# A table of products of weights, built through DRAM and then built on TensorE alone

## What is computed

```python
def _cin_layer(x0, x, kernel):
    W = kernel.reshape(m, h_prev, kernel.shape[1])
    return jnp.einsum('bmd,bhd,mho->bod', x0, x, W)
x = x0
finals = []
for k in (k1, k2, k3):
    x = _cin_layer(x0, x, k)
    finals.append(jnp.sum(x, axis=-1))
logit = jnp.concatenate(finals, axis=-1) @ kf
```

## Time and profile before

| | us |
|---|---|
| median of 3 runs (311.8 to 312.88) | 311.81 |
| the profiled execution | 312.8 |
| span of its instructions | 311.0 |
| PE busy in the span | 294.1 |
| POOL, DVE, ACT busy | 221.9, 196.8, 179.2 |
| contractions (L568) | 228.7 |

### The profile page before, as it was taken

One profiled execution on the slowest core, in us unless ns is written; L12 is line 12 of the kernel. 1 busy time (PEld: TensorE's weight loads), 2 busy tenths in 40 slices (PEclk: granted clock), 3 DMA queues, 4 the chain that ended last, 5 costly groups with the idle time before them and its releaser, 6 DMA issues.

```text
span 311.0 us, 7703 instructions
## 1 busy us (share of the span) xinstructions
PE 294.1 (95%) x3018; PEld 84.2 (27%) x3018; DVE 196.8 (63%) x215; ACT 179.2 (58%) x195; POOL 221.9 (71%) x131
## 2 busy tenths in 40 slices
PE   7249989999999999999999999999999999999995
PEld 2032322222222222222222222222222222222231
DVE  0555657766665667766665667776665667776631
ACT  1336537756574756766574756766574756677511
POOL 0334877969698797969697896979697896979700
PEclk9756999999999999999999999999999999999999
DMA  6998999999998969799697979799797979620100
GB/s 210 401 346 243 386 365 355 383 394 327 415 301 357 301 266 342 309 315 334 273 307 270 301 268 329 301 334 329 283 300 278 297 269 316 257 70 2 34 2 1
DMA packets 18632, 86.86 MB, mean 279 GB/s; under 512 B 3899, under 2 KB 4155, under 8 KB 9915
## 3 DMA queue, kind: packets, MB, share of 16 engines
q1 hardware_dynamic: 15880, 78.10, 68.5%
q10 hardware_dynamic: 2707, 8.57, 11.2%
q0 software_dynamic: 32, 0.00, 0.0%
HBM read 86.13 MB, written 0.53 MB: 279 GB/s over the span
## 4 chain that ended last, share of the span: by engine, by line
PE 87%; DMA 5%; DVE 3%; ACTq 2%; ACT 1%; issue 1%; POOL 1%; SPq 0%; POOLq 0%
PE acc L568 69%; PE acc L576 10%; PE rot L554 8%; DMA feat<-u_rows 3%; DMA u<-k3p 2%; ACTq L336 1%; DVE split L465 1%; DVE prod L490 1%; ACT prod L287 0%; ACT split L299 0%; ACTq L191 0%; POOL split L400 0%; PE acc L584 0%; PE acc L622 0%; ACT ysb L304 0%
## 5 line engine op out<-in xcount | busy, mean ns | idle before, releaser
L568 PE MATMUL acc<-prod,w 128*32 128x512 f32 x2048 | 228.7, 598 | 4.2 <-ACT prod L287 2.9
L390 POOL TENSOR_TENSOR prod<-u,v 128x1024 f32<-128x1024 f32 x64 | 152.6, 2385 | 23.2 <-PE acc L568 17.3
L568 PEld LDWEIGHTS acc<-prod,w 128*32 128x32 f32 x2048 | 63.5, 110 | 152.4 <-issue 135.3
L490 DVE TENSOR_TENSOR prod<-rot,u 128x1024 f32<-128x1024 f32 x64 | 77.7, 1215 | 6.3 <-PE rot L554 4.4
L287 ACT ACTIVATE prod<-rot 128x1024 f32<-128x1024 f32 x64 | 65.2, 1021 | 24.8 <-PE rot L554 17.4
L496 DVE TENSOR_TENSOR xy<-acc,ysb 128x512 f32<-128x512 f32 x32 | 22.1, 691 | 89.3 <-ACT ysb L304 89.3
L490 DVE TENSOR_TENSOR prod<-rot,v 128x1024 f32<-128x1024 f32 x64 | 77.6, 1213 | 0.0
L304 ACT ACTIVATE ysb<-acc,kf 128x512 f32<-128x512 f32 x32 | 22.0, 687 | 84.3 <-PE acc L576 54.0
L291 ACT ACTIVATE feat<-u 96x2048 f32<-96x2048 f32 x32 | 60.9, 1903 | 0.0
L396 POOL TENSOR_TENSOR low<-xc,split 128x512 f32<-128x512 f32 x30 | 35.1, 1170 | 32.7 <-ACT split L295 32.7
L400 POOL TENSOR_TENSOR split<-low,split 128x512 bf16<-128x512 f32 x30 | 34.9, 1164 | 5.0 <-ACT split L299 4.7
(11 more groups left out here) (35 smaller groups left out, 21.6 us busy)
## 6 DMA issues: line engine op xcount, KB each, us to landing
u<-u_rows SPq DMA_DIRECT2D x30, 1024.0 KB, 4.9
v<-v_rows SPq DMA_DIRECT2D x30, 1024.0 KB, 8.7
xc<-x_chunks SPq DMA_DIRECT2D x32, 256.0 KB, 10.0
feat<-u_rows ACTq DMA_DIRECT2D x30, 256.0 KB, 7.4
u<-u_rows SPq DMA_DIRECT2D x4, 512.0 KB, 11.7
v<-v_rows SPq DMA_DIRECT2D x4, 512.0 KB, 12.8
u<-k3p SPq DMA_DIRECT2D x2, 512.0 KB, 5.4
...
```

The lines of the kernel that those rows point to most:

```text
L390: nc.gpsimd.tensor_tensor(prod[p][:, UV, pair(half)], us[n][:, pair(half)], vs[n][:, pair(half)], ALU.mult).then_inc(uv_ready, 2)
L490: nc.vector.tensor_tensor(prod[p][:, t, pair(half)], rot[:, pair(half)], r[n][:, pair(half)], ALU.mult).then_inc(products_ready, 1)
L568: mm = nc.tensor.matmul(acc[p][h][quad(c), :], w[:, t, h * G:(h + 1) * G], prod[p][:, t, chunk(c)], start=(t == first), stop=(first is Non ...
```

## The change

T is made in another layout and never leaves the core. TensorE multiplies `k2s` (as weights, 32 columns for each c) by `vk`: 32 matmuls of 64 columns give T with g on the partitions, four values of c side by side in the four groups of 32 partitions (`t_ps`). VectorE and ScalarE copy it in four pieces (`place_t`) to `tt`, a table of 95 x 64 places in the second buffer of `prod`; it holds zeros elsewhere, which GpSimd fills in with one MEMSET of 6080 elements as its first instruction. A weight table of a tile is a diagonal of `tt`, read in steps of 65 elements. `tables_of_t` uses each diagonal (`diagonal`) as weights against a 32 x 32 unit matrix, and so gathers, transposes and adds left and right in PSUM (`sum_ps`): 54 matmuls of 32 columns. One ScalarE copy puts the sum in `w`. The diagonal for the single squares and the linear part are gathered by two more such matmuls in `fold(1)`.

The code of slabs 0 and 1 is changed along with it. All fixes come before the first contraction, slab 1's rotation comes after the whole x1 half of slab 0, and slab 1's products and slab 2's split are made in step 0 as in the loop. Slab 1 is split by GpSimd. `xc` of slab 0 is loaded ahead of `k2t`, `pick` ahead of `kf`; the loads of slabs 1 to 3 have a new order, and no DMA of the table is left on SyncE, ScalarE or GpSimd.

```diff
-WRAP = 2 * M
+WRAP = 2 * M - 1
+ORDERS = (FIRST, {t: pair[::-1] for t, pair in FIRST.items()})
-                fold[q, i, m] += 1
+                fold[q, i, m] -= 1
+        tt = prod[1][:, UW:, :].rearrange("p t n -> p (t n)")[:, 0:(M + WRAP) * 2 * M]
+        t_places = tt.rearrange("p (c a) -> p c a", a=2 * M)
-        vt_ps, v_ps = acc[0][1][:, 0:H1], acc[1][1][:, 0:M]
-        t_ps = [acc[0][1][2 * M * n:2 * M * n + M + 1, :] for n in range(2)]
+        vt_ps, v_ps, t_ps = acc[0][1][:, 0:H1], acc[1][1][:, 0:WRAP], acc[0][0]
+        sum_ps = acc[1][1][:, P:2 * P].rearrange("p (t g) -> p t g", g=G)
+        def diagonal(pair, q, turn):
+            (c, dc), (a, da) = pair
+            at = ((0 if turn else M) + c + dc * q) * 2 * M + a + da * q
+            return tt[:, at:at + (M - 1) * (2 * M + 1) + 1:2 * M + 1]
+        def place_t(copy, n):
+            for j in (2 * n, 2 * n + 1):
+                copy(t_places[quad(j), M + j:2 * M:Q, :], t_ps[quad(j), :].rearrange("p (c a) -> p c a", a=2 * M)
+                     ).then_inc(tt_ready[n], 1)
...
+            load_xc(0, 0)
             sp.dma_start(k2s, k2t).then_inc(k2_in, 16)
-            load_xc(0, 0)
             sp.dma_start(k1s[:], k1g).then_inc(k1_in, 16)
...
             load_halves(0, 0)
+            load_halves(1, 1)
+            place_fields(sp, 0, 0)
+            load_halves(1, 0)
             load_xc(2, 2)
-            place_fields(sp, 0, 0)
-            load_halves(1, 1)
-            load_halves(1, 0)
+            load(2, 2)
             place_fields(sp, 1, 1)
-            sp.wait_ge(t_out, 32)
-            sp.dma_start(tl[:, UW, :], table(*FIRST[UW])).then_inc(t_in, 16)
-            sp.dma_start(tr[:, UW, :], table(*FIRST[UW][::-1])).then_inc(t_in, 16)
-            sp.dma_start(tl[:, WW, :], table(*FIRST[WW])).then_inc(t_in, 16)
-            sp.dma_start(tr[:, WW, :], table(*FIRST[WW][::-1])).then_inc(t_in, 16)
-            load(2, 2)
             load_xc(3, 3)
+            sp.wait_ge(t_ready, 1)
             load(3, 3)
...
-            act.dma_start(vk[:, M:M + 1], kf[M:M + H1, :]).then_inc(kf2_in, 16)
+            act.dma_start(pick32[:], pick).then_inc(pick_in, 16)
+            act.dma_start(vk[:, WRAP:], kf[M:M + H1, :]).then_inc(kf2_in, 16)
...
             act.dma_start(kf1[:], bass.AP(tensor=kf.tensor, offset=0, ap=[[0, CHUNKS], [1, M], [1, 1]])
                           ).then_inc(kf1_in, 16)
-            act.dma_start(pick32[:], pick).then_inc(pick_in, 16)
             act.wait_ge(xc_in[0], 16)
             split_high(0, 0, 0)
+            split_mid(0, 0)
             act.wait_ge(t_ready, 1)
-            nc.scalar.copy(ts[:, CHUNK:], t_ps[1]).then_inc(ts_ready, 1)
-            act.wait_ge(ts_ready, 2)
-            store_t(act, 0)
-            store_t(act, 1)
-            split_mid(0, 0)
+            act.wait_ge(tt_cleared, 1)
+            place_t(nc.scalar.copy, 1)
+            act.wait_ge(rot_ready, 1)
+            square_w(0, 0, 0)
             act.wait_ge(xc_in[1], 16)
             split_high(1, 1, 1)
-            split_mid(1, 1)
-            act.wait_ge(rot_ready, 1)
-            square_w(0, 0, 0)
             act.wait_ge(products_ready, 2)
             square_w(0, 0, 1)
-            act.wait_ge(xc_in[2], 16)
-            split_high(2, 0, 2)
-            act.wait_ge(t_out, 32)
-            act.dma_start(tl[:, VW, :], table(*FIRST[VW])).then_inc(t_in, 16)
-            act.wait_ge(cleared, 2)
-            act.dma_start(tr[0:HALFWAY.start, VW, :], table(*FIRST[VW][::-1], count=Q - 1)).then_inc(t_in, 16)
-            act.dma_start(tl[:, UV, :], table(*FIRST[UV])).then_inc(t_in, 16)
-            act.dma_start(tr[:, UV, :], table(*FIRST[UV][::-1])).then_inc(t_in, 16)
-            act.wait_ge(cleared, 1)
-            act.dma_start(wf[quad(3), :], ts[M:M + 1, :]).then_inc(lin_in, 16)
+            act.wait_ge(sum_ready, 1)
+            nc.scalar.copy(w[:, :, G:2 * G], sum_ps).then_inc(w_ready[1], 1)
+            split_mid(1, 1)
             for half in range(2):
                 act.wait_ge(first_in[0][half], 32)
-            split_mid(2, 0)
             square_fields(0, 0, 0)
             act.wait_ge(kf1_in, 16)
...
-                    if not isinstance(s, int) or 1 <= s < SLABS - 2:
+                    if not isinstance(s, int) or s < SLABS - 2:
...
+            nc.gpsimd.memset(tt, 0.0).then_inc(tt_cleared, 1)
             pool.wait_ge(k1_in, 16)
-            add_tables(0, k1s[:, 0:TILES, :], k1s[:, TILES:2 * TILES, :])
+            nc.gpsimd.tensor_tensor(w[:, :, 0:G], k1s[:, 0:TILES, :], k1s[:, TILES:2 * TILES, :], ALU.add
+                                    ).then_inc(w_ready[0], 1)
             for half in (1, 0):
                 pool.wait_ge(first_in[0][half], 32)
                 multiply_uv(0, 0, half)
-            pool.wait_ge(t_out, 32)
-            pool.dma_start(td[quad(2), :], bass.AP(tensor=t_tab.tensor, offset=0,
-                                          ap=[[(WRAP + 1) * G, M], [1, G]])).then_inc(td_in, 16)
-            split_low(2, 0, 2)
-            split_last(2, 0)
-            pool.wait_ge(t_in, 16 * 8)
-            add_tables(1, tl[:], tr[:])
+                if half == 1:
+                    split_low(1, 1, 1)
+            split_last(1, 1)
...
-            dve.wait_ge(t_ready, 1)
-            nc.vector.tensor_copy(ts[:, 0:CHUNK], t_ps[0]).then_inc(ts_ready, 1)
             split_low(0)
             dve.wait_ge(pick_in, 16)
             nc.vector.tensor_copy(picks[:], pick32[:]).then_inc(picks_ready, 1)
             split_last(0)
+            dve.wait_ge(t_ready, 1)
+            dve.wait_ge(tt_cleared, 1)
+            place_t(nc.vector.tensor_copy, 0)
             dve.wait_ge(rot_ready, 1)
             multiply_w(0, 0, 0, (1,))
             subtract_fixes(0)
-            split_low(1)
             multiply_w(0, 0, 0, (0,))
-            split_last(1)
-            fold_squares(0, quad(0), k1s[quad(0), 2 * TILES, :])
-            dve.wait_ge(rot_ready, 2)
-            multiply_w(1, 1, 1, (1,))
             subtract_fixes(1)
-            dve.wait_ge(td_in, 16)
-            fold_squares(1, quad(2), td[quad(2), :])
-            multiply_w(1, 1, 1, (0,))
+            dve.wait_ge(wf_cleared, 1)
+            dve.wait_ge(fold_ready[0], 1)
+            nc.vector.tensor_tensor(wf[quad(0), :], k1s[quad(0), 2 * TILES, :], fold_ps[0], ALU.add
+                                    ).then_inc(wf_ready[0], 1)
+            dve.wait_ge(fold_ready[1], 1)
+            nc.vector.tensor_copy(wf[2 * M:, :], rest_ps).then_inc(wf_ready[1], 1)
...
+            def tables_of_t():
+                for t in range(TILES):
+                    parts = [[(order[t], turn) for n, order in enumerate(ORDERS) if (n, t, q) != (1, VW, Q - 1)
+                              for turn in range(1 + (order[t][0][0] + order[t][0][1] * q > 0))] for q in range(Q)]
+                    for k in range(max(len(of) for of in parts)):
+                        for q, of in enumerate(parts):
+                            if k < len(of):
+                                mm = nc.tensor.matmul(sum_ps[quad(q), t, :], diagonal(of[k][0], q, of[k][1]),
+                                                      kzs[:, 2 * M:3 * M], start=(k == 0), stop=(k == len(of) - 1),
+                                                      skip_group_check=True)
+                mm.then_inc(sum_ready, 1)
             def fold(h):
                 pe.wait_ge(fixed[h], 2)
-                nc.tensor.matmul(fold_ps[h], fixs[:, 4 * P:], w[:, WW, h * G:(h + 1) * G], start=True, stop=True
-                                 ).then_inc(fold_ready[h], 1)
+                mm = nc.tensor.matmul(fold_ps[h], fixs[:, 4 * P:], w[:, WW, h * G:(h + 1) * G], start=True,
+                                      stop=(h == 0), skip_group_check=True)
+                if h == 1:
+                    nc.tensor.matmul(fold_ps[1], diagonal((ZERO, ZERO), 0, 0), kzs[:, 2 * M:3 * M], start=False,
+                                     stop=True, skip_group_check=True)
+                    mm = nc.tensor.matmul(rest_ps[M:, :], t_places[:, M:2 * M, WRAP], kzs[:, 2 * M:3 * M], start=True,
+                                          stop=True, skip_group_check=True)
+                mm.then_inc(fold_ready[h], 1)
...
-            nc.tensor.matmul(v_ps, vts[:], kzs[:, 2 * M:], start=True, stop=True).then_inc(v_done, 1)
+            nc.tensor.matmul(v_ps, vts[:], kzs[:, 2 * M:2 * M + WRAP], start=True, stop=True).then_inc(v_done, 1)
             pe.wait_ge(v_ready, 1)
             pe.wait_ge(kf2_in, 16)
             pe.wait_ge(k2_in, 16)
-            for n in range(2):
-                mm = nc.tensor.matmul(t_ps[n], vk[:], k2s[:, n * CHUNK:(n + 1) * CHUNK], start=True, stop=True)
+            for c in range(M):
+                at = c // Q * 2 * M
+                mm = nc.tensor.matmul(t_ps[quad(c % Q), at:at + 2 * M], k2s[:, c * G:(c + 1) * G], vk[:],
+                                      start=True, stop=True, skip_group_check=True)
```

(17 more changed lines are left out.)

71 lines of the change are left out of this document (25 added, 46 removed).

## The result

The changed kernel takes 308.83 us (median of 5 runs, 308.59 to 309.75), the kernel before 311.81 beside it. The ratio is 0.9912, with a 95% interval of 0.9885 to 0.9938: 3.0 us or 1% less. The same two kernels, run again on another occasion, gave 308.35 (6 runs) against 312.15 (11 runs), ratio 0.9876 (0.9848 to 0.9904). The ratios leave out an execution that lies over 1.5% above the fastest of its kernel; here that is a single one, the profiled execution of e_fill. The forecast was 6.1 us less, so the direction was right and the size was twice too large.

The account below looks back on a forecast made before the run. TensorE was taken as the bound, busy from 50 us on, with gains only ahead of the loop: slab 1's contraction 4.8 us earlier and 1.3 from the feature row, minus 6.1, giving 305.7 us; range 303.5 to 312.3.

Parts of the forecast that it names:

- The waits of 5.5 and 2.9 us: TensorE's waits for VectorE's last split of slab 0 (5.5) and ScalarE's squares of slab 0 (2.9): both forecast to go.
- the wait ahead of rotate(2): Ahead of slab 1's contraction: TensorE waits for GpSimd's split of slab 2, forecast as 1.9 us.
- the wait on the feature row: TensorE's wait of 1.3 us behind 43 us for the DMA of slab 2's feature row: forecast to go.
- the chain of the split: Split of slab s + 2 hangs on the rotation of s + 1: 6.5 us from rotation's end to GpSimd's split_last.
- The price of a small matmul: T and tables: 0.026 us from record to record; 0.052 for the tables at 1.2 GHz.
- the range of 6.4 to 13.9: GpSimd's MEMSET of 6080 elements: bounds from VectorE's MEMSET and GpSimd's product; lower end taken, hidden by loads and T.
- what is late next. A new wait of 1.9 us: Step before rotate(2): slab 2's split comes at 31.3, TensorE is done at 29.4, slab 1's contraction begins at 32.1.
- The baseline: Whole kernel: profiled execution 312.8 us, median 1.0 below it at 311.81; the forecast for the median starts from 311.8.
- R1: Start: tables and fixes don't bring back 2.4 GHz; clock stays down until the contractions; 311.6 us, chance 0.19.
- R2: Tables: diagonal weights read slowly, 0.052 us a record at 2.4 GHz, 0.104 at 1.2; 309.9 us, shared chance 0.17.
- R3: GpSimd's MEMSET takes 13.9 us, so place_t and tables start later: +2.5, 308.2 us; shared chance 0.17.
- R4: Start: DRAM trip was covered (0.2 us), TensorE only gets 54 more matmuls; no chance beyond R1's.

Follow-up runs that it names:

- e_fill: Changed kernel with 12 matmuls of 512 columns on zeros in TensorE's wait ahead of rotate(2): median 307.89 us (8 runs).
- e_xc2: Changed kernel with the load of slab 2's xc put ahead of slab 1's halves: 308.69 us (7 runs).
- e_shift: Changed kernel with 20 matmuls of 32 columns on zeros ahead of the first matmuls of V: 308.76 us (4 runs).
- e_copy: Changed kernel with TensorE's code 19 instructions shorter ahead of the tables and ScalarE's copy of their sum ahead of its second square of slab 0: 308.74 us.
- e_xc2_fill: Changed kernel with slab 2's xc loaded ahead of slab 1's halves and 8 matmuls on zeros ahead of rotate(2): 307.69 us, ratio 0.9862 to the kernel before.
- e_split2: Changed kernel with slab 2's xc loaded ahead of slab 1's halves and slab 2 split ahead of the loop: 307.62 us, ratio 0.9857 to the kernel before.
- e_all: Changed kernel with the edits of e_split2 and e_copy together: 307.12 us (6 runs), ratio 0.9859 to the kernel before.
- e_few_tables: Changed kernel with only 16 of the 54 matmuls of the tables: 307.85 us (4 runs).
- e_before: The kernel before, unedited, profiled again: profiled execution 312.55 us, median of 14 runs beside it 311.74.

## Why the prediction was half right

*What held.* The waits of 5.5 and 2.9 us went, the wait ahead of rotate(2) came, the wait on the feature row went, and where xc was there in time the chain of the split took 6.4 us from rotation to rotation, as read from the loop (e_xc2, e_shift, e_copy). The rows foretold slab 1's contraction at 32.1, and it came at 32.52. That it came so near is luck: TensorE reached the wait at 28.5 instead of 29.4, stood 0.8 longer and then took 0.6 longer in rotate(2).

*What cancelled on the way.* T began at 8.9 (9.8 forecast) and took 1.10 us and not 1.9: 64 records at 0.013 us each, half the lower bound. The tables took 3.8 us and not 4.5, but made up otherwise: 99 records in 1.99 us at 1.2 GHz, 0.020 each where 0.052 was taken, and a gap of 1.5 us that no row had announced. The price of a small matmul was taken from sixteen records with 128 columns, 0.026 us; with 64 columns it is 0.013, and with the 32 columns of the tables 0.019 to 0.020 at either level of the clock, so columns alone don't set it. The MEMSET took 5.16 us, below the range of 6.4 to 13.9. The clock fell once in slab 0's first contraction (5.24 us for 29 records), where I had it back for good.

*The step that failed* is "what is late next. A new wait of 1.9 us". It was priced as idle time alone. In the trace of before, a wait of TensorE was followed by 1.2 GHz; the prediction used that for the start and forgot it for the wait that it had itself added. It cost 0.6 us in rotate(2) and 1.15 in the contraction. The wait was also 0.8 longer, because ScalarE's split had to wait for slab 2's xc, which landed at 25.8, behind slab 1's halves, and which I had not checked. Of eight profiles in which TensorE stood empty for 1.8 to 3.2 us between 27 and 33 us, seven show the slow level right behind; e_copy, with 1.82 us, does not, and why is open. The four in which that wait was filled or gone (e_fill, e_xc2_fill, e_split2, e_all) all keep 2.4 GHz. In whole executions this price can hardly be seen: those four lie 0.9 to 1.7 us below 308.83 and 0.5 to 1.2 below 308.35, but so does e_few_tables, 307.85, which has the slow stretch, and e_copy, without it, gains nothing.

*The sum.* At the features of slab 1 the changed kernel was ahead by 45.46 - 40.60 = 4.9 us instead of 6.1. It ends ahead by 311.0 - 306.8 = 4.2. The 0.7 in between went in the loop, where the prediction held that nothing in the change touches the work: 4.85 were left at rotate(5) (64.74 against 59.89), 4.48 at rotate(6) (72.50 against 68.02), which waited 0.30 us for GpSimd's split and did not before, and the rest went in steps of under 0.1. Behind rotate(5) ScalarE's two issues of feature rows start 0.59 us after its copy of y ends, and its first square 0.81 after the rotation; before it was 0.21 and 0.43. That is the size of the step, and why the issues come late was not tried. The loss is no accident of one execution: from the start of rotate(3) to the end of the span it is 263.6 or 263.7 us in both profiles of the kernel before, and 264.2 to 264.4 in all eleven of the changed kernel and those made from it. All that they differ in lies ahead of rotate(3).

*The baseline.* The last 1.2 us, from 4.2 by the profiles to 3.0 by the medians, is no property of the edit: the profiled execution of before lay 1.0 above its median (0.8 in e_before), that of after 0.2 below. The forecast moved both by the same 1.0. On the second occasion the medians differed by 3.8. So of the 3.1 us by which 6.1 was too much, some 1.2 are the clock and the longer wait, less what the early start gave back, 0.7 the loop, and 1.2 the reading of a profiled execution as a typical one. The last share is the least certain.

*The rivals.* R1 (1.2 GHz until the contractions) did not come about: PEclk is 0.50, 1.00, 0.50 and 1.00 again by 22 us. R2 (slow diagonals) fell as a price: a record took 0.020 us at 1.2 GHz, where R2 had 0.104. Loads of weights with steps of 65 elements took a median of 163 ns there, against 164 for neighbours. But at 2.4 GHz the diagonals are slower. The last two of these lines are e_xc2_fill's loads for T, which read neighbours, and for its tables, both at that level:

```profile
L569 PEld LDWEIGHTS acc<-kzs,prod x108: 133/163/189, 12.0 to 15.6; 128*32 128x32 f32 x108
```

```profile
L616 PEld LDWEIGHTS acc<-vk,v x64: 106/110/110, 8.9 to 9.8; 128*32 128x32 f32 x64
L570 PEld LDWEIGHTS acc<-kzs,prod x108: 133/158/168, 11.9 to 15.9; 128*32 128x32 f32 x108
```

So 158 ns against 110, and 0.018 us from record to record (1.81 us for 99) where T, with twice the columns, has 0.013. The diagonals hardly gain from the higher clock; by an estimate from these rows that is some 108 x 0.005 or 0.5 us. The Trainium skill (SBUF — State Buffer, Door 1: The DMA port swizzle) says that each access that goes to a new line of 16 bytes pays. The trace agrees in direction at 2.4 GHz; no run here changes the step alone. R3 (a slow MEMSET) fell. R4 was given no chance as a rival; its premise, that the trip was covered, was true only as long as nothing else got faster.
